# Column softmax with side projections in pieces of 128 columns, its sums copied one unit later, and the heads' inputs in another order with deeper rings

## The chip, the cores and the metric

One NeuronCore of one Trainium2 chip runs the whole program in one launch. The metric is the device time of one execution in microseconds; the time of a version is the median of its runs. Engines are named as in the profile: PE (TensorE, with PEld for its weight loads), DVE (VectorE), ACT (ScalarE), POOL (GpSimd) and SP (SyncE, here the queue that issues the DMAs).

## The reference, cut to what matters

Four transformer-like layers over `x` of 2 x 2048 tokens by 128 channels. The change touches two places of them.

```python
# layer 2: inputs of 16 heads of width 8, queries and keys rotated; six heads dot, four hyperbolic, six cosine
q = apply_rot(q, cos, sin); k = apply_rot(k, cos, sin)
tq = sqrt(1.0 / curv + sum(q * q, -1)); tk = sqrt(1.0 / curv + sum(k * k, -1))
qn = q / max(norm(q), 1e-12)

# layer 3, first part: a softmax over the QUERY axis, so that sums over keys are needed of its columns
scores = einsum('neax,nebx->neab', Q, K); A = softmax(scores, axis=2)
Out = einsum('neab,neax->neax', A, V)
# layer 3, second part: its projections need only xn
q = xn @ Wq; k, v = split(xn @ Wkv)
```

## The kernel before, in words

Activations stay in on-chip memory as [128 channels, 4096 tokens]. Each stage is a block in which every engine has its own list of instructions, and semaphores order them across engines. Within one engine the order is the order of the code, so an instruction that waits holds up all behind it.

**head_inputs** (from L973) makes layer 2's queries and keys: 2 jobs (q, k) of 8 chunks of 512 tokens, so 16 steps `n`. A step runs: PE projects twice (L1007, L1008); DVE rotates (L1066 to L1068); ACT squares (L1028); PE sums squares over a head (L1014); ACT takes a root by Ln and Exp (`time_of`, L1034, L1035); DVE clips (L1075); ACT takes the inverse root (`root`, L1039, L1040); DVE scales (L1080 to L1083). Then the float32 result is split in three bf16 parts: ACT copies the high part (L1044), DVE subtracts (`rests`, L1089), ACT copies the middle (L1049), DVE subtracts (`lows`, L1093). The same split of `time` runs on ACT (L1045, L1051) and POOL (L1104, L1108). The order on each engine is a software pipeline: in slot `k` an engine does, one behind the other, the listed parts, each for step `k - lag` (`slot`). Rings (`n % 4`, `n % 2`) hold the intermediate results, and waits on an older step guard them. SP stores q's parts when its 8 steps are done, and k's at the end.

**column_softmax_sums** (from L1726) treats 32 heads (2 batches x 16) of 16 tiles (`ST`). A tile is 128 keys against 2048 queries, in two units `h` of 1024 columns. For a unit PE makes scores (L1831, into a ring of three PSUM buffers, `RING`), DVE takes the negated maximum (L1964), ACT takes the exponential with its sum (L1885), and this frees the PSUM buffer. Eleven tiles later (`LAG`) PE adds the tile, weighted, into `r_ps` (`add_up`, L1842). After the 16 tiles of a head DVE copies `r_ps` out (`collect`, L1957), and the next head's first `add_up` waits for that copy. Per group of 8 tiles small operations of DVE, POOL and ACT make the weights (L1970, L1916 to L1924, L1951).

Between them PE makes, for one 128-token tile per head, three **side projections** (`side`, L1855 for kinds 0 and 1, L1858 for kind 2) for the second part of layer 3, into one PSUM bank of 512 columns. They stand behind tile 3, 8 and 13 of a head (`SIDE_AT`). ACT copies each out one tile later (L1892), SP stores them. PE's list for a tile is: scores of unit 0, scores of unit 1, `add_up`, and after three tiles a side projection.

Before the first head DVE clears `cs_q` and `cs_k` (L1941, L1942); SP waits for this before it loads the first heads (L1787). Of the 128 partitions 96 are then overwritten.

Of the kernel before, what the change touches and what calls it, by code (L numbers as in the profile page):

```python
# [972 lines left out]
def head_inputs(nc, xn, W, cos, sin, jobs):  # L973
# [7 lines left out]
    with Scope(nc, "hi") as sc:  # L981
        (projected, rotated, squared, summed, timed, clipped, rooted, scaled, act_step, high, rested, mid, low, t_high, t_rested, t_mid,
         t_low, stored, own) = (sc.sem(n) for n in names)
        a, time, f = (sc.sb(n, [128, 4, CH]) for n in ("a", "time", "f"))
# [15 lines left out]
        with nc.Block() as block:  # L1000
# [19 lines left out]
            def _(act):  # L1020
# [3 lines left out]
                def square(n):  # L1024
                    act.wait_ge(rotated, n + 1)
                    if n >= 2:
                        act.wait_ge(summed, n - 1)
                    act.activation(sq[:, n % 2, :], a[:, n % 4, :], ACT.Square).then_inc(squared, 1)  # L1028

                def time_of(n):  # L1030
                    act.wait_ge(summed, n + 1)
                    if n >= 4:
                        act.wait_ge(t_rested, n - 3)
                    steps(act.activation(time[:, n % 4, :], n_ps[:, n % 2, :], ACT.Ln, bias=W["inv_c"]))  # L1034
                    act.activation(time[:, n % 4, :], time[:, n % 4, :], ACT.Exp, scale=0.5).then_inc(timed, 1)  # L1035
# [6 lines left out]
                def highs(n):  # L1042
                    act.wait_ge(scaled, n + 1)
                    act.activation(part(parts, n, 0), a[:, n % 4, :], ACT.Copy).then_inc(high, 1)  # L1044
                    act.activation(part(t_parts, n, 0), time[:, n % 4, :], ACT.Copy).then_inc(t_high, 1)  # L1045
# [7 lines left out]
                for k in range(total + 4):  # L1053
                    slot(k, ((square, 0), (time_of, 1), (root, 2), (highs, 3), (mids, 4)))

            @block.vector
            def _(dve):
                steps = Steps(dve, own)

                def rotate(n):  # L1060
                    j, c = steps_of[n]
                    at = slice((c % CPB) * CH, (c % CPB + 1) * CH)
                    dve.wait_ge(projected, n + 1)
                    if n >= 4:
                        dve.wait_ge(rested, n - 3)
                    steps(dve.tensor_tensor(turned[:, n % 2, :], t_ps[:, n % 2, :], sin[:, at], ALU.mult))  # L1066
                    steps(dve.tensor_tensor(a[:, n % 4, :], a_ps[:, n % 2, :], cos[:, at], ALU.mult))
                    dve.tensor_tensor(a[:, n % 4, :], a[:, n % 4, :], turned[:, n % 2, :], ALU.add).then_inc(rotated, 1)  # L1068
# [8 lines left out]
                def scale(n):  # L1077
                    job = jobs[steps_of[n][0]]
                    if job["times_c"]:
                        steps(dve.tensor_scalar(time[:, n % 4, :], time[:, n % 4, :], W["c"], None, ALU.mult))  # L1080
                    dve.wait_ge(rooted, n + 1)
                    steps(dve.tensor_scalar(f[:, n % 4, :], f[:, n % 4, :], job["cosine"], job["base"], ALU.mult, ALU.add))
                    dve.tensor_tensor(a[:, n % 4, :], a[:, n % 4, :], f[:, n % 4, :], ALU.mult).then_inc(scaled, 1)  # L1083

                def rests(n):
# [3 lines left out]
                    dve.tensor_tensor(rest[:, n % 4, :], a[:, n % 4, :], part(parts, n, 0), ALU.subtract).then_inc(rested, 1)  # L1089
# [5 lines left out]
                for k in range(total + 4):  # L1095
                    slot(k, ((rotate, 0), (clip, 1), (scale, 2), (rests, 3), (lows, 4)))

            @block.gpsimd
            def _(pool):
                def rests(n):  # L1100
# [3 lines left out]
                    pool.tensor_tensor(t_rest[:, n % 4, :], time[:, n % 4, :], part(t_parts, n, 0), ALU.subtract).then_inc(t_rested, 1)  # L1104
# [5 lines left out]
                for k in range(total + 4):  # L1110
                    slot(k, ((rests, 3), (lows, 4)))
# [614 lines left out]
def column_softmax_sums(nc, qd, kd, r_dram, xn, side_weights, side_dram):  # L1726
# [8 lines left out]
    with Scope(nc, "cs") as sc:  # L1735
# [11 lines left out]
        SIDE_AT = (3, 8, 13)  # L1747
# [30 lines left out]
        with nc.Block() as block:  # L1778
            @block.sync
            def _(sp):  # L1780
# [23 lines left out]
                sp.wait_ge(cleared, 2)  # L1804
# [16 lines left out]
            def _(pe):  # L1821
# [25 lines left out]
                def side(seg, e, kind):  # L1847
                    if seg.it is not None or e or kind:
                        pe.wait_ge(side_copied, seg.count(3, 3 * e + kind))
                    if kind == 0:  # L1850
                        pe.wait_ge(side_staged, seg.count(1, e + 1))
                    tile = side_x[:, e % 2, :]
                    if kind < 2:
                        for j in range(4):
                            mm = pe.matmul(side_ps[:, j * 128:(j + 1) * 128], side_weights[kind][:, j * 128:(j + 1) * 128], tile,  # L1855
                                           start=True, stop=True)
                    else:
                        mm = pe.matmul(side_ps[:, :], tile, side_weights[2], start=True, stop=True)  # L1858
                    mm.then_inc(side_made, 1)

                def emit(seg):
                    for t in seg.tiles():
# [4 lines left out]
                        if t % ST in SIDE_AT:  # L1867
                            side(seg, t // ST, SIDE_AT.index(t % ST))
# [7 lines left out]
            def _(act):  # L1876
                def emit(seg):
                    for t in seg.tiles():
# [8 lines left out]
                        if t % ST - 1 in SIDE_AT:  # L1887
                            kind, e = SIDE_AT.index(t % ST - 1), t // ST
# [11 lines left out]
            def _(pool):  # L1900
                PER_GROUP = 1
# [38 lines left out]
            def _(dve):  # L1940
                dve.memset(q[:, :, :], 0.0).then_inc(cleared, 1)  # L1941
                dve.memset(k[:, :, :], 0.0).then_inc(cleared, 1)  # L1942
# [16 lines left out]
                def emit(seg):  # L1959
                    for t in seg.tiles():  # L1960
                        for h in range(2):
# [11 lines left out]
                            if t % ST == LAG - 1 and h == 0 and (seg.it is not None or t >= ST):  # L1973
# [649 lines left out]
```

## Time and profile before

| What | us |
|---|---|
| median of 3 runs | 7267.65 (7259.87 to 7271.13) |
| the profiled execution | 7271.85, its span 7270.1 |
| head_inputs, first DVE rotation to last subtraction | 2083.0 to 2232.6 of the span |
| column_softmax_sums, first scores to last copy of sums | 4187.3 to 5516.2 of the span |

The span is read in stages, since each has its own limit: the busy shares of a stage come from the table by stretches, the waits from the view of who waited for whom, and the order of single instructions from the timeline. A bracket at a timeline row's end is the idle time of that engine just before it, and what ended that. "x8" is a run of eight instructions merged in one row. Granted clock 1.0 is TensorE at 2.4 GHz, 0.5 at 1.2 GHz.

### The profile page before, as it was taken

To read this page: it belongs to the slowest core of one execution; us is meant where nothing else is said; L and a number is where in the kernel's file an instruction comes from. 1 tells how busy PE (TensorE), PEld (TensorE's weight loads), DVE (VectorE), ACT (ScalarE), POOL (GpSimd) and SP (SyncE) were. 2 spreads that over 40 slices of the span, in tenths; PEclk is the share of its full clock that TensorE was granted. 3 is DMA by queue.
4 is the path that set the end of the run, shared out by engine and by line. 5 is a ranking of instruction groups with operands and counts; after the bars stand their busy time and mean duration, and the time that the engine had idled before them with its cause. 6 is when DMAs were issued, how large, how long until landed. Compare 5 with 4: busy or idle time off the path is not lost. (4 is left out here: it accounts for less than half of the span.)

```text
span 7270.1 us, 82198 instructions
## 1 busy us (share of the span) xinstructions
PE 5207.4 (72%) x23371; PEld 1824.1 (25%) x23371; DVE 5160.6 (71%) x6074; ACT 3896.3 (54%) x5386; POOL 1562.8 (21%) x983
## 2 busy tenths in 40 slices
PE   5466677978854868833333367777775999999999
PEld 2122233433311222200000111111112344444443
DVE  4688845444455666489798489999994688888887
ACT  4333321242444534689799489999993333333333
POOL 0244400000011000000000000000000577777776
PEclk7678788988967988955555689999997999999999
DMA  0000000000003112000000233332331110111110
GB/s 17 4 0 0 0 13 12 0 15 0 0 16 106 34 29 51 17 11 0 13 0 0 73 36 41 38 43 36 44 36 21 44 30 21 24 30 30 30 30 12
DMA packets 204967, 174.58 MB, mean 24 GB/s; under 512 B 145346, under 2 KB 186446, under 8 KB 196526
## 3 DMA queue, kind: packets, MB, share of 16 engines
q1 hardware_dynamic: 204606, 170.09, 12.4%
q8 instruction: 187, 3.06, 0.2%
q14 instruction: 174, 1.43, 0.1%
HBM read 118.80 MB, written 51.23 MB: 23 GB/s over the span
## 5 line engine op out<-in xcount | busy, mean ns | idle before, releaser
L1964 DVE TENSOR_REDUCE cs_neg<-cs_s_ps 128x1 f32<-128x1024 f32 x1024 | 1182.4, 1215 | 112.2 <-PE cs_s_ps L1831 96.1
L1885 ACT ACTIVATE cs_E<-cs_s_ps,cs_neg 128x1024 f32<-128x1024 f32 x1024 | 1134.4, 1120 | 135.9 <-DVE cs_neg L1964 135.9
L2237 ACT ACTIVATE da_P<-da_P 128x1024 f32<-128x1024 f32 x512 | 541.2, 1057 | 930.9 <-DVE da_P L2312 912.1
L2278 POOL TENSOR_TENSOR da_psum<-da_psum,da_P 128x1024 f32<-128x1024 f32 x384 | 904.9, 2357 | 366.7 <-ACT da_P L2237 334.0
L2295 DVE TENSOR_REDUCE da_mx<-da_s_ps 128x1 f32<-128x1024 f32 x512 | 623.9, 1220 | 198.2 <-PE da_s_ps L2161 198.1
L1831 PE MATMUL cs_s_ps<-cs_q,cs_k 64*128 64x512 bf16 x2048 | 390.5, 396 | 372.2 <-ACT cs_E L1885 343.6
L1259 PE MATMUL hypb_o_ps<-hypb_P,hypb_vq 128*32 128x512 f32 (+3 forms) x640 | 193.7, 933 | 607.5 <-DVEq L1649 403.6
L2312 DVE TENSOR_TENSOR da_P<-da_s_ps,da_lift 128x1024 f32<-128x1024 f32 x512 | 600.6, 1215 | 3.5 <-PE da_s_ps L2165 3.4
L2161 PE MATMUL da_s_ps<-da_k,da_q 64*128 64x512 f32 x2048 | 553.1, 618 | 20.8 <-DMA da_v<-vf 15.2
L1842 PE MATMUL cs_r_ps<-cs_E,cs_w 128*32 128x512 f32 x4096 | 551.5, 613 | 1.4 <-POOL cs_w L1924 1.4
L2175 PE MATMUL da_o_ps<-da_P,da_v 128*64 128x512 f32 x2048 | 495.9, 605 | 0.0
L2165 PE MATMUL da_s_ps<-da_q,da_k 64*128 64x512 f32 x2048 | 482.9, 590 | 0.0
L478 PE MATMUL scan_y_ps<-scan_hC,consts 128*128 128x512 f32 x512 | 346.6, 814 | 145.5 <-POOL scan_hC L514 143.6
L514 POOL TENSOR_TENSOR scan_hC<-scan_h,scan_c_sb 128x1024 f32<-128x1024 f32 x128 | 301.2, 2353 | 642.6 <-DVE scan_h L537 642.6
L1461 DVE TENSOR_REDUCE cos_mu<-cos_m_ps 128x1 f32<-128x512 f32 (+1 forms) x480 | 262.3, 604 | 134.4 <-PE cos_m_ps L1420 91.4
L500 ACT ACTIVATE scan_dA<-mamba_dts,mamba_wt 128x1024 f32 x128 | 147.1, 1150 | 341.2 <-DVE scan_h L537 332.8
L1449 ACT ACTIVATE cos_P<-cos_s_ps 128x1024 f32<-128x1024 f32 (+1 forms) x240 | 203.6, 893 | 210.9 <-PE cos_s_ps L1398 118.3
L1831 PEld LDWEIGHTS cs_s_ps<-cs_q,cs_k 64*128 64x128 bf16 x2048 | 90.8, 93 | 884.3 <-ACT cs_E L1885 833.1
L1449 ACT ACTIVATE dot_P<-dot_s_ps 128x1024 f32<-128x1024 f32 (+1 forms) x240 | 202.0, 893 | 191.4 <-PE dot_s_ps L1398 124.2
L1104 POOL TENSOR_TENSOR hi_t_rest<-hi_time,hi_t_parts 128x512 f32<-128x512 f32 x16 | 20.8, 1300 | 1243.8 <-ACT hi_t_parts L1045 1243.7
L2165 PEld LDWEIGHTS da_s_ps<-da_q,da_k 64*128 64x128 f32 x2048 | 197.8, 187 | 240.0 <-issue 224.1
L1461 DVE TENSOR_REDUCE dot_mu<-dot_m_ps 128x1 f32<-128x512 f32 (+2 forms) x320 | 174.9, 605 | 103.0 <-PE dot_m_ps L1420 65.7
(437 smaller groups left out, 8904.0 us busy)
## 6 DMA issues: line engine op xcount, KB each, us to landing
da_q<-qf SPq DMA_DIRECT2D x32, 512.0 KB, 8.7
da_k<-kf SPq DMA_DIRECT2D x32, 512.0 KB, 10.6
cs_q<-q_parts SPq DMA_DIRECT2D x384, 32.0 KB
cs_k<-k_parts SPq DMA_DIRECT2D x384, 32.0 KB
qf<-cs_side_sb SPq DMA_DIRECT2D x32, 256.0 KB, 3.4
kf<-cs_side_sb SPq DMA_DIRECT2D x32, 256.0 KB, 5.3
vf<-cs_side_sb SPq DMA_DIRECT2D x32, 256.0 KB, 5.8
da_v<-vf SPq DMA_DIRECT2D x16, 512.0 KB, 11.9
```

Of the source, the lines that this page charges most:

```text
L1461: dve.tensor_reduce(mu[:, x % 2, i, o // CH:o // CH + 1], m_ps[:, u % M_RING, 0:w], AX.X, ext["op"]).then_inc(reduced, 1)
L1831: mm = pe.matmul(s_ps[:, seg.slot(u, RING, 2), c * CH:(c + 1) * CH], k[half, p, i * 128:(i + 1) * 128], q[half, p, at], start=True, stop=True)
L1842: mm = pe.matmul(r_ps[32 * a:32 * a + 32, :], weight, E[:, seg.slot(t, E_RING), a // 2, (a % 2) * CH:(a % 2 + 1) * CH], start=(i == 0), st ...
L1885: act.activation(E[:, seg.slot(t, E_RING), h, :], s_ps[:, seg.slot(u, RING, 2), :], ACT.Exp, bias=neg[:, g, j, h:h + 1], accum_out=z[:, g, ...
L1964: dve.tensor_reduce(neg[:, g, j, h:h + 1], s_ps[:, seg.slot(u, RING, 2), :], AX.X, ALU.max, negate=True).then_inc(maxed, 1)
L2161: mm = pe.matmul(s_ps[:, slot, c, :], q[half(c), p, tile * 128:(tile + 1) * 128], k[half(c), p, part * CH:(part + 1) * CH], start=True, st ...
L2165: mm = pe.matmul(s_ps[:, slot, c, :], k[half(c), p, kt * 128:(kt + 1) * 128], q[half(c), p, (quad % CPB) * CH:(quad % CPB + 1) * CH], star ...
L2175: mm = pe.matmul(o_ps[half(c), :], v[:, p, 2 * u + c, :], P[:, g % RING, c, :], start=(u == 0), stop=(u == UNITS - 1))
L2237: act.activation(P[:, g % RING, :, :], P[:, g % RING, :, :], ACT.Exp).then_inc(exped, 1)
L2278: pool.tensor_tensor(psum[:, :, :], psum[:, :, :], P[:, g % RING, :, :], ALU.add).then_inc(pooled, 1)
L2295: dve.tensor_reduce(mx[:, g // UNITS % 2, g % UNITS // 2, g % 2:g % 2 + 1], s_ps[:, slot, :, :].rearrange("p c n -> p (c n)"), AX.X, ALU.m ...
L2312: dve.tensor_tensor(P[:, g % RING, :, :], s_ps[:, slot, :, :], lift[:, quad % 2, :].unsqueeze(1).to_broadcast([128, 2, CH]), ALU.add).then ...
```

## The change

In head_inputs `a` gets 6 buffers for 4 and `time` 5 for 4, and the order within a slot and the lags change on ACT, DVE and POOL. In column_softmax_sums a side projection is made in pieces of 128 columns: one piece behind each of two tiles, two behind the third, so over tiles 3 to 5, 7 to 9 and 11 to 13. Kind 2, one matmul of 512 columns before, becomes four of 128. ACT copies the bank out in the tile of the last piece, no longer one tile later. DVE's `collect` moves behind the second unit of tile 10, from behind the first. The clearing takes only the partitions 32 to 63 and 96 to 127, `cs_q` by DVE and `cs_k` by POOL.

```diff
-        a, time, f = (sc.sb(n, [128, 4, CH]) for n in ("a", "time", "f"))
+        a, time, f = (sc.sb(n, [128, k, CH]) for n, k in (("a", 6), ("time", 5), ("f", 4)))
...
# ACT
-                for k in range(total + 4):
-                    slot(k, ((square, 0), (time_of, 1), (root, 2), (highs, 3), (mids, 4)))
+                for k in range(total + 5):
+                    slot(k, ((time_of, 1), (highs, 3), (square, 0), (mids, 5), (root, 1)))
...
# DVE
-                for k in range(total + 4):
-                    slot(k, ((rotate, 0), (clip, 1), (scale, 2), (rests, 3), (lows, 4)))
+                for k in range(total + 7):
+                    slot(k, ((rests, 4), (rotate, 0), (lows, 7), (clip, 1), (scale, 2)))
...
# POOL
-                for k in range(total + 4):
-                    slot(k, ((rests, 3), (lows, 4)))
+                for k in range(total + 2):
+                    slot(k, ((rests, 0), (lows, 2)))
...
-        SIDE_AT = (3, 8, 13)
+        SIDE_AT = {at + n: (kind, ((0,), (1,), (2, 3))[n]) for kind, at in enumerate((3, 7, 11)) for n in range(3)}
...
-                sp.wait_ge(cleared, 2)
+                sp.wait_ge(cleared, 4)
...
# PE
-                def side(seg, e, kind):
-                    if seg.it is not None or e or kind:
-                        pe.wait_ge(side_copied, seg.count(3, 3 * e + kind))
-                    if kind == 0:
-                        pe.wait_ge(side_staged, seg.count(1, e + 1))
+                def side(seg, e, kind, quarters):
+                    if quarters[0] == 0:
+                        if seg.it is not None or e or kind:
+                            pe.wait_ge(side_copied, seg.count(3, 3 * e + kind))
+                        if kind == 0:
+                            pe.wait_ge(side_staged, seg.count(1, e + 1))
                     tile = side_x[:, e % 2, :]
-                    if kind < 2:
...
-                    else:
-                        mm = pe.matmul(side_ps[:, :], tile, side_weights[2], start=True, stop=True)
-                    mm.then_inc(side_made, 1)
+                    for j in quarters:
+                        part = slice(j * 128, (j + 1) * 128)
+                        weight = side_weights[kind][:, part]
+                        mm = pe.matmul(side_ps[:, part], *((tile, weight) if kind == 2 else (weight, tile)), start=True, stop=True)
+                    if quarters[-1] == 3:
+                        mm.then_inc(side_made, 1)
...
# ACT, behind the two exponentials of tile t
-                        if t % ST - 1 in SIDE_AT:
-                            kind, e = SIDE_AT.index(t % ST - 1), t // ST
+                        if t % ST in SIDE_AT and SIDE_AT[t % ST][1][-1] == 3:
+                            kind, e = SIDE_AT[t % ST][0], t // ST
...
# POOL
+                for base in (32, 96):
+                    pool.memset(k[base:base + 32, :, :], 0.0).then_inc(cleared, 1)
+                pool.wait_ge(cleared, 4)
...
# DVE
-                dve.memset(q[:, :, :], 0.0).then_inc(cleared, 1)
-                dve.memset(k[:, :, :], 0.0).then_inc(cleared, 1)
+                for base in (32, 96):
+                    dve.memset(q[base:base + 32, :, :], 0.0).then_inc(cleared, 1)
...
-                            if t % ST == LAG - 1 and h == 0 and (seg.it is not None or t >= ST):
+                            if t % ST == LAG - 1 and h == 1 and (seg.it is not None or t >= ST):
```

How this moves instructions, at the places that matter. The first is PE's list round tiles 7 to 9 of the second head of column_softmax_sums, before (-) and now (+); L1831 are scores, L1842 is `add_up`, L1855 and L1857 are side projections (a row of four L1831 is one tile).

```order
 L1831 MATMUL cs_s_ps<-cs_q,cs_k 128x512 x4
 L1842 MATMUL cs_r_ps<-cs_E,cs_w 32x512 x4
+L1857 MATMUL cs_side_ps<-cs_side_x,l3w_wt 128x128
 L1831 MATMUL cs_s_ps<-cs_q,cs_k 128x512 x4
 L1842 MATMUL cs_r_ps<-cs_E,cs_w 32x512 x4
-L1855 MATMUL cs_side_ps<-cs_side_x,l3w_wt 128x128 x4
+L1857 MATMUL cs_side_ps<-cs_side_x,l3w_wt 128x128
 L1831 MATMUL cs_s_ps<-cs_q,cs_k 128x512 x4
 L1842 MATMUL cs_r_ps<-cs_E,cs_w 32x512 x4
+L1857 MATMUL cs_side_ps<-cs_side_x,l3w_wt 128x128 x2
```

Four matmuls in a row ahead of the next tile's scores have become one, one and two, behind three tiles. The second place is DVE in head_inputs, one slot of the k job in the middle of the stage. Before:

```order
L1066 TENSOR_TENSOR hi_turned<-hi_t_ps,l2p_sin 128x512
L1067 TENSOR_TENSOR hi_a<-hi_a_ps,l2p_cos 128x512
L1068 TENSOR_TENSOR hi_a<-hi_a,hi_turned 128x512
L1075 TENSOR_SCALAR hi_f<-hi_n_ps 128x512
L1082 TENSOR_SCALAR hi_f<-hi_f,l2w_wt 128x512
L1083 TENSOR_TENSOR hi_a<-hi_a,hi_f 128x512
L1089 TENSOR_TENSOR hi_rest<-hi_a,hi_parts 128x512
L1093 TENSOR_TENSOR hi_parts<-hi_rest,hi_parts 128x512
```

And now the same slot:

```order
L1089 TENSOR_TENSOR hi_rest<-hi_a,hi_parts 128x512
L1066 TENSOR_TENSOR hi_turned<-hi_t_ps,l2p_sin 128x512
L1067 TENSOR_TENSOR hi_a<-hi_a_ps,l2p_cos 128x512
L1068 TENSOR_TENSOR hi_a<-hi_a,hi_turned 128x512
L1093 TENSOR_TENSOR hi_parts<-hi_rest,hi_parts 128x512
L1075 TENSOR_SCALAR hi_f<-hi_n_ps 128x512
L1082 TENSOR_SCALAR hi_f<-hi_f,l2w_wt 128x512
L1083 TENSOR_TENSOR hi_a<-hi_a,hi_f 128x512
```

The instructions are the same eight. The clip L1075 is still one step behind the rotation, but ACT now begins its slot with that step's `time_of` and has no square of the newest step ahead of it; a step's last subtraction L1093 comes three slots later than before.

## Rows read from the trace of the kernel before

**Rows 1.** The page: busy us (share of the span) of each engine.
```profile
PE 5207.4 (72%) x23371; PEld 1824.1 (25%) x23371; DVE 5160.6 (71%) x6074; ACT 3896.3 (54%) x5386; POOL 1562.8 (21%) x983
```

**Rows 2.** Stretches: head_inputs, column softmax; us, busy PE, PEld, DVE, ACT, POOL, clock, DMA.
```profile
2082.00:2232.00 150.00, 69.41 (x94) 24.65 (x92) 113.89 (x136) 81.20 (x144) 43.85 (x31) 0.68 0.12 44
4188.00:5520.00 1332.00, 980.02 (x6718) 245.22 (x6714) 1210.31 (x1184) 1208.95 (x2208) 63.55 (x287) 0.98 0.30 39
```

**Rows 3.** Who waited for whom, 4210 to 5500 us: total us, times, longest.
```profile
DVE cs_neg L1964 <- PE cs_s_ps L1831: 73.0, 100, 3.4
...
DVE cs_r_sb L1957 <- PE cs_r_ps L1842: 14.8, 31, 0.5
```

**Rows 4.** Timeline of DVE over one head, 4600 to 4670 us: start, us, instruction, idle before.
```profile
4609.60 9.34 DVE L1964 TENSOR_REDUCE cs_neg<-cs_s_ps 128x1 f32<-128x1024 f32 x8 [0.79 <-PE cs_s_ps L1831]
...
4622.05 1.23 DVE L1964 TENSOR_REDUCE cs_neg<-cs_s_ps 128x1 f32<-128x1024 f32 x1 [0.63 <-PE cs_s_ps L1831]
...
4626.02 0.69 DVE L1957 COPY cs_r_sb<-cs_r_ps 128x512 f32<-128x512 f32 x1 [0.42 <-PE cs_r_ps L1842]
4626.63 8.00 DVE L1964 TENSOR_REDUCE cs_neg<-cs_s_ps 128x1 f32<-128x1024 f32 x7
4635.34 4.62 DVE L1964 TENSOR_REDUCE cs_neg<-cs_s_ps 128x1 f32<-128x1024 f32 x4 [0.70 <-PE cs_s_ps L1831]
...
4666.60 0.69 DVE L1957 COPY cs_r_sb<-cs_r_ps 128x512 f32<-128x512 f32 x1 [0.51 <-PE cs_r_ps L1842]
```

**Rows 5.** Timeline of PE round a side projection, same head.
```profile
4632.53 0.39 PE L1831 MATMUL cs_s_ps<-cs_q,cs_k 64*128 64x512 bf16 x2 [0.56 <-ACT cs_E L1885]
4632.85 1.06 PE L1842 MATMUL cs_r_ps<-cs_E,cs_w 128*32 128x512 f32 x8
4633.85 1.12 PE L1858 MATMUL cs_side_ps<-l3w_wt,cs_side_x 128*128 128x512 f32 x2
4634.91 0.61 PE L1831 MATMUL cs_s_ps<-cs_q,cs_k 64*128 64x512 bf16 x4
```

**Rows 6.** Timeline of ACT: a copy of a side projection and exponentials behind it.
```profile
4613.09 0.58 ACT L1892 ACTIVATE cs_side_sb<-cs_side_ps 128x512 f32<-128x512 f32 x1
4613.57 1.11 ACT L1885 ACTIVATE cs_E<-cs_s_ps,cs_neg 128x1024 f32<-128x1024 f32 x1
...
4614.66 1.12 ACT L1885 ACTIVATE cs_E<-cs_s_ps,cs_neg 128x1024 f32<-128x1024 f32 x1
```

**Rows 7.** Groups of DVE in head_inputs: busy, mean ns, idle before, releaser.
```profile
L1093 DVE TENSOR_TENSOR hi_parts<-hi_rest,hi_parts 128x512 bf16<-128x512 f32 x16 | 25.1, 1576 | 0.0
L1089 DVE TENSOR_TENSOR hi_rest<-hi_a,hi_parts 128x512 f32<-128x512 f32 x16 | 24.4, 1524 | 0.0
...
L1075 DVE TENSOR_SCALAR hi_f<-hi_n_ps 128x512 f32<-128x512 f32 x16 | 11.1, 691 | 29.0 <-ACT hi_time L1035 29.0
...
L1082 DVE TENSOR_SCALAR hi_f<-hi_f,l2w_wt 128x512 f32<-128x512 f32 x16 | 9.6, 597 | 4.3 <-ACT hi_f L1040 4.3
```

**Rows 8.** Timeline of head_inputs, DVE and POOL, one step; then DVE near the stage's end.
```profile
2149.56 1.27 POOL L1104 TENSOR_TENSOR hi_t_rest<-hi_time,hi_t_parts 128x512 f32<-128x512 f32 x1 [6.80 <-ACT hi_t_parts L1045]
2149.74 1.64 DVE L1089 TENSOR_TENSOR hi_rest<-hi_a,hi_parts 128x512 f32<-128x512 f32 x1
...
2150.80 1.59 POOL L1108 TENSOR_TENSOR hi_t_parts<-hi_t_rest,hi_t_parts 128x512 bf16<-128x512 f32 x1
2151.30 1.64 DVE L1093 TENSOR_TENSOR hi_parts<-hi_rest,hi_parts 128x512 bf16<-128x512 f32 x1
...
2228.81 0.68 DVE L1089 TENSOR_TENSOR hi_rest<-hi_a,hi_parts 128x512 f32<-128x512 f32 x1
```

**Rows 9.** Timeline: DVE's clearing, SP's first load behind it, a clearing by POOL.
```profile
4164.85 1.76 DVE L1942 MEMSET cs_k<- 128x2048 uint32 x1 [0.38 <-issue]
4166.64 0.32 SPq L1787 DMA_DIRECT2D cs_q<-q_parts  x1
...
2266.50 3.51 POOL L1375 MEMSET cos_vq<- 128x4096 f32 x1 [32.88 <-POOLq L957]
```

More of the change, by code:

```diff
@@ L1027, in square @@
                         act.wait_ge(summed, n - 1)
-                    act.activation(sq[:, n % 2, :], a[:, n % 4, :], ACT.Square).then_inc(squared, 1)
+                    act.activation(sq[:, n % 2, :], a[:, n % 6, :], ACT.Square).then_inc(squared, 1)
                 def time_of(n):
                     act.wait_ge(summed, n + 1)
[L1032 to L1035, printed above, removed]
+                    if n >= 5:
+                        act.wait_ge(t_rested, n - 4)
+                    steps(act.activation(time[:, n % 5, :], n_ps[:, n % 2, :], ACT.Ln, bias=W["inv_c"]))
+                    act.activation(time[:, n % 5, :], time[:, n % 5, :], ACT.Exp, scale=0.5).then_inc(timed, 1)
                 def root(n):
@@ L1043, in highs @@
                     act.wait_ge(scaled, n + 1)
-                    act.activation(part(parts, n, 0), a[:, n % 4, :], ACT.Copy).then_inc(high, 1)
-                    act.activation(part(t_parts, n, 0), time[:, n % 4, :], ACT.Copy).then_inc(t_high, 1)
+                    act.activation(part(parts, n, 0), a[:, n % 6, :], ACT.Copy).then_inc(high, 1)
+                    act.activation(part(t_parts, n, 0), time[:, n % 5, :], ACT.Copy).then_inc(t_high, 1)
                 def mids(n):
@@ L1079, in scale @@
                     if job["times_c"]:
-                        steps(dve.tensor_scalar(time[:, n % 4, :], time[:, n % 4, :], W["c"], None, ALU.mult))
+                        steps(dve.tensor_scalar(time[:, n % 5, :], time[:, n % 5, :], W["c"], None, ALU.mult))
                     dve.wait_ge(rooted, n + 1)
                     steps(dve.tensor_scalar(f[:, n % 4, :], f[:, n % 4, :], job["cosine"], job["base"], ALU.mult, ALU.add))
-                    dve.tensor_tensor(a[:, n % 4, :], a[:, n % 4, :], f[:, n % 4, :], ALU.mult).then_inc(scaled, 1)
+                    dve.tensor_tensor(a[:, n % 6, :], a[:, n % 6, :], f[:, n % 4, :], ALU.mult).then_inc(scaled, 1)
                 def rests(n):
@@ L1088, in rests @@
                         dve.wait_ge(low, n - 3)
-                    dve.tensor_tensor(rest[:, n % 4, :], a[:, n % 4, :], part(parts, n, 0), ALU.subtract).then_inc(rested, 1)
+                    dve.tensor_tensor(rest[:, n % 4, :], a[:, n % 6, :], part(parts, n, 0), ALU.subtract).then_inc(rested, 1)
                 def lows(n):
@@ L1103, in rests @@
                         pool.wait_ge(t_low, n - 3)
-                    pool.tensor_tensor(t_rest[:, n % 4, :], time[:, n % 4, :], part(t_parts, n, 0), ALU.subtract).then_inc(t_rested, 1)
+                    pool.tensor_tensor(t_rest[:, n % 4, :], time[:, n % 5, :], part(t_parts, n, 0), ALU.subtract).then_inc(t_rested, 1)
                 def lows(n):
@@ L1867, in emit @@
                         if t % ST in SIDE_AT:
-                            side(seg, t // ST, SIDE_AT.index(t % ST))
+                            side(seg, t // ST, *SIDE_AT[t % ST])
                 segments(pe, emit)
```

11 lines of the change are left out of this document (4 added, 7 removed).

## The prediction

> **What bounds the kernel now.** I read the page first: no engine is busy for more than 72% of the span [rows 1], so the limit changes from stage to stage, and only the two stages that the change edits matter. The table by stretches gives them [rows 2]. In column_softmax_sums DVE is busy for 1210.31 us and ACT for 1208.95 us of 1332, 91% each, and PE for 980.02. In head_inputs DVE is busy for 113.89 of 150 us, and the others for much less. So DVE is nearly the bound in both, and what can be won is its idle time, plus what lengthens its instructions.
>
> Next, the waits of column_softmax_sums [rows 3]: DVE waits 73.0 us for scores, in 100 waits, and 14.8 us in 31 waits ahead of its copy of the sums. The timeline says where [rows 4]. A head takes 40.58 us (from the copy at 4626.02 to the next at 4666.60), and DVE stops in it four times: 0.79, 0.63 and 0.70 us ahead of a maximum, one behind each side projection, and 0.42 to 0.51 us ahead of the copy. PE's timeline shows why [rows 5]: `add_up` holds it for 1.00 us (4632.85 to 4633.85), the side projection for 1.06 more, and only then can the scores of the next tile start.
>
> In head_inputs [rows 7] DVE waits 29.0 us ahead of the clip L1075, always for ACT's `time_of`, and 4.3 us ahead of L1082 for ACT's root. The subtractions L1089 and L1093 take 1.5 us each on average.
>
> **Part 1, the pieces.** A side projection delays the next scores by 1.06 us and costs DVE 0.71 us (mean of the three): 0.35 us are absorbed by the ring of three score buffers. Over 32 heads the three waits are 32 x 3 x 0.71 = 68 us; the 73.0 us [rows 3], less a few of other kinds, say the same. A quarter of a projection takes 1.06 / 4 = 0.265 us. A single piece is below the 0.35 absorbed and costs DVE nothing; what hides it is the time that the scores lie ready in the ring, and without that it would cost 0.265. Two pieces take 0.53 and leave 0.53 - 0.35 = 0.18 us. So three times 0.18 remain per head, 17 us in all, and the part gives 68 - 17 = **51 us**. Kind 2, cut from one matmul of 512 columns into four, has no row in that form; kinds 0 and 1 always had the form of four, and their waits (0.79, 0.63) stand beside the 0.70 of kind 2. So I take the same length. The number of PE's projections and their work stay as they are. The new matmuls wait for nothing new: kind 1 starts at tile 7 and kind 0 was copied behind tile 5.
>
> **Part 2, the sums one unit later.** At tile 10 DVE reaches the copy before PE has ended the `add_up` that it needs, since this stands in PE's list behind both scores of the tile. One unit of maximum takes 8.00 / 7 = 1.14 us [rows 4], more than the 0.42 to 0.51 us waited. The wait goes: 14.8 us x 32 / 31 = **15 us**. What is late next is PE's `add_up` of the next head's first tile, which waits for the copy; it stands behind both scores of tile 11, and these need the exponentials of tile 10, so it comes at about the time at which the copy ends. I cost it at nothing; without that cover it would cost up to the copy's 0.69 us less 0.35, 11 us in all.
>
> **Part 3, ACT's copy in the same tile.** The copy holds ACT for 0.48 us (4613.09 to 4613.57) [rows 6], and the scores behind it come later by that. It shows only as small gaps inside DVE's run: eight maxima in 9.34 us, from which (9.34 - 1.23) / 7 = 1.16 us each, against (8.00 - 1.23) / 6 = 1.13 where no copy lies [rows 4]. That is 0.2 us per copy, 20 us over 96 copies. Now it lies in the gap that the two last pieces leave. I take **8 us** of the 20. The new wait, of ACT for the last piece, has the next tile's exponentials behind it. From the scores of unit 1 the last piece ends 0.32 + 1.00 + 0.53 = 1.85 us later [rows 5]; a maximum (1.23) and an exponential (1.11) stand between those scores and the copy, so it waits for nothing.
>
> Together 51 + 15 + 8 = 74 us, 2.3 per head, to 38.3. The floor is DVE's own work per head: 32 maxima at 1.13, the copy 0.61 (4626.02 to 4626.63), and about 0.4 for the four small operations of the groups, 37.2 us. So these parts can give at most 3.4 x 32 = 109 us. At ACT's fastest pace, 1.09 us per exponential (4613.57 to 4614.66), it needs 34.9 + 3 x 0.48 + 0.3 = 36.6, so it does not bind before DVE. From below: if the ring absorbed nothing of a single piece and only 0.2 of a double one, the waits would be 3 x (0.265 x 2 + 0.33) = 2.6 per head, more than the 2.1 of now; parts 1 to 3 would give about 0. I take 74, since the 0.35 is measured on all three waits, and as the low end of the range half of it, 37.
>
> **Part 4, head_inputs.** The instructions are the same; the order changes. ACT now begins a slot with `time_of` of the last step, whose sum of squares is long there, and DVE clips it behind a rotation and two subtractions. So the 29.0 us go, and the 4.3 with them, since the root now has a whole slot. Against this stands the longer tail: the last subtraction comes 7 slots behind the rotation instead of 4, with little in each; three more slots of one 0.68 us subtraction [rows 8] come to 2 us. Gain 33.3 - 2.3 = **31 us** of 150. The two extra ring buffers pay for the longer lags and cost nothing by themselves. SP's stores of q start a few us sooner or later beside other work; those of k stay at the end as before.
>
> What POOL does to DVE stays open. L1089 takes 1.64 us while POOL's L1104 runs beside it, and 0.68 us where POOL is idle [rows 8]; the two subtractions thus lose 1.92 us a step, 31 us in all. In the new order POOL's two meet other instructions. I leave the loss as it is: the same POOL work meets a DVE that is now almost always busy. If it all fell on instructions that don't mind, the gain would be 31 + 31 = 62; if DVE stood still for all of POOL's 1.27 + 1.59 us a step [rows 8], the loss would grow by 0.94 x 16 = 15 us, and the gain fall to 16.
> The Trainium skill's page "SBUF — State Buffer" ("Who interferes with whom") says that a DVE instruction with two SBUF inputs and a GpSimd instruction that reads SBUF exclude each other for the whole instruction, while one with a single SBUF input is left alone. By that rule the L1066, L1067 and L1075, which read PSUM, would be free, and the sum would lie between those two ends. The trace agrees in the 1.64 against 0.68 us; that DVE gets something done within POOL's 2.84 us (2149.56 to 2152.39) speaks against a lock that is never yielded.
>
> **Part 5, the clearing.** DVE's two are as long as before if only the elements per partition count. POOL's have no row at 32 partitions in bf16. The nearest is 3.51 us for 4096 elements per partition [rows 9]; at that, two take 7.0 us from about 4162.9, and SP starts at 4170 in place of 4166.64: **+3.4 us**, on the path, since PE waits for these loads. If bf16 went at twice the rate it would be 0. As nothing in the trace excludes a gain, the lower end is -1.8, one of DVE's 1.76 us.
>
> **Sum:** -74 - 31 + 3.4 = -102 us, so 7271.85 - 102 = 7170 for a profiled execution. The median before is 4.2 us below that execution, so I forecast 7166.
>
> **The rivals.**
> (a) *The floor comes sooner.* Column softmax gains 37 us, because ACT, as busy as DVE, takes over the waits, or because single pieces aren't absorbed. For: 91% busy on both [rows 2]. Against: ACT's pace of 1.09 us behind a copy. Time: -37 - 31 + 3.4 = -65, 7203. Chance 0.14.
> (b) *POOL locks DVE.* DVE stands for all of POOL's 2.86 us a step, since its six instructions on on-chip data alone meet them: -74 - 16 + 3.4 = -87, 7181; chance 0.12, as DVE was seen to get on beside POOL. It is what the rule of the Trainium skill's page "SBUF — State Buffer" would come to at its strictest.
>  The mirror case, POOL's work meeting free instructions: -74 - 62 + 3.4 = -133, 7135; chance 0.08.
> (c) *Slower: each change of PE from `add_up` to a piece has a fixed price.* If what costs DVE 0.71 us is not the projection's length but the interruption, nine tiles cost 6.4 us per head where three cost 2.1: +137 us, less 15 and 31, plus 3.4: +94, 7362. It decides from the point where 9 x 32 x w - 68, with w the wait per tile with a piece, exceeds 15 + 31 - 3.4, that is from w = 0.38 us. Against: PE goes from `add_up` to L1858 and on to the scores without idle [rows 5]. Chance 0.03.
> (d) *It doesn't do what it says:* the sides' gaps stay, as the clip's wait moves to another instruction of DVE and the double pieces to the old wait; within 0.2% of now. Chance 0.03.
>
> The forecast itself, with part 1 to 3 between 55 and 95 and part 4 between 22 and 45, has 0.60, and reaches from 7133 to 7194. The range takes in (b) whole and most of (a): 7130 to 7205. Faster by over 0.2% (14.5 us, about what a measurement of this kernel can tell from no change) has 0.94, within it 0.03, slower 0.03.
>
> **What would show it.** Right: a head of 38.3 us from copy to copy; no idle above 0.1 us behind tiles 3, 4, 7, 8, 11 and 12, and about 0.2 behind 5, 9 and 13; none ahead of the copy of sums; in head_inputs no wait of DVE at the clip, and a stage of 119 us for 149.6; SP's first load 7 us behind the start of the clearing. Wrong: heads of 39.5 us or more with waits spread over nine tiles, a wait of PE at `add_up` for the copy, or a DVE in head_inputs that is busy throughout but with more instructions at 1.6 us.

## The result, and the profile after

The changed kernel takes 7211.99 us (median of 4 runs, 7206.25 to 7221.84), the kernel before beside it 7263.76: a ratio of 0.9933, 95% interval 0.9913 to 0.9952. That is faster, by 52 us, but only half of the forecast 102, and outside the range. (One of the nine executions of the kernel before beside runs 11 and 12 took 14498.82 us, at a granted clock of 0.415, and is in no ratio.) The profiled executions differ by 7270.1 - 7219.8 = 50.3 us of span. Cut at the first and last instructions on each stage's tiles, the difference is:

| stretch | before | after | difference | forecast |
|---|---|---|---|---|
| start to head_inputs | 2083.0 | 2087.2 | +4.2 | 0 |
| head_inputs, to the last use of its parts | 157.1 | 121.5 | -35.6 | -31 |
| from there to the clearing | 1922.6 | 1913.4 | -9.2 | 0 |
| clearing to the first scores | 24.6 | 26.8 | +2.2 | +3.4 |
| first scores to last copy of sums | 1329.0 | 1270.7 | -58.3 | -74 |
| to the first scores of dense_attention | 146.3 | 150.9 | +4.6 | 0 |
| scores of dense_attention | 1583.5 | 1625.3 | **+41.8** | 0 |
| tail | 24.0 | 24.0 | 0 | 0 |

dense_attention, which the diff does not touch, gives back 42 us. The first line of part 1 of the page, and the instruction queue in part 3 (187 packets before):

```profile
PE 5250.3 (73%) x23563; PEld 1868.7 (26%) x23563; DVE 5158.4 (71%) x6074; ACT 3904.0 (54%) x5386; POOL 1568.6 (22%) x985
...
q8 instruction: 192, 3.15, 0.2%
```

The page counts 192 matmul records more for PE [rows 1]: kind 2 is now four matmuls in place of one, so three more in each of 32 heads, and each is two records. The list of who waited for whom, PE from 5500 us on, has a line that is missing before:

```profile
PE da_s_ps L2164 <- issue: 33.3, 9, 6.5
```

Here are its two costliest places in one pass of the loop, in PE's timeline (start, us, instruction, idle before):

```profile
6184.32 1.13 PE L2164 MATMUL da_s_ps<-da_k,da_q 64*128 64x512 f32 x4 [2.29 <-issue]
6185.28 1.89 PE L2168 MATMUL da_s_ps<-da_q,da_k 64*128 64x512 f32 x8
6193.63 2.08 PE L2164 MATMUL da_s_ps<-da_k,da_q 64*128 64x512 f32 x4 [6.46 <-issue]
```

The same pair stands at 6392.66 and 6401.98, at 6600.97 and 6609.46, and at 6808.75 and 6817.80: at four of the loop's five back-edges, at its head and again 12 matmul records later. PE waits there for nothing that the profile shows; the experiments say for what. The stretch table adds the clock (columns: us, busy PE, PEld, DVE, ACT, POOL, granted clock, DMA share, GB/s):

```profile
6170.00:6182.00 12.00, 12.00 (x57) 4.56 (x55) 10.05 (x12) 4.61 (x5) 9.34 (x5) 1.00 0.02 3
6192.00:6196.00 4.00, 2.37 (x6) 0.80 (x8) 0.25 (x1) 0.00 (x0) 1.99 (x1) 0.50 0.90 201
```

Behind the idle time the clock is at 0.50, 1.2 GHz, and the four records of L2164 take 2.08 us for 1.13. So 33.3 of the 41.8 us are the waits, and the clock behind them makes up the rest: over the four pairs, the rows that ran at the low clock in whole or in part (L2164, L2168, L2178) are 9.6 us longer than the same rows at 1.00, which would make 42.9. The 0.90 of DMA share is the loads of the next head, which SP starts at the same place.

The column softmax, DVE over one head (answers to [rows 4]):

```profile
4644.04 0.68 DVE L1960 COPY cs_r_sb<-cs_r_ps 128x512 f32<-128x512 f32 x1
4644.64 11.78 DVE L1967 TENSOR_REDUCE cs_neg<-cs_s_ps 128x1 f32<-128x1024 f32 x10
...
4660.06 10.38 DVE L1967 TENSOR_REDUCE cs_neg<-cs_s_ps 128x1 f32<-128x1024 f32 x9
4670.74 4.62 DVE L1967 TENSOR_REDUCE cs_neg<-cs_s_ps 128x1 f32<-128x1024 f32 x4 [0.29 <-PE cs_s_ps L1831]
...
4680.40 2.36 DVE L1967 TENSOR_REDUCE cs_neg<-cs_s_ps 128x1 f32<-128x1024 f32 x2 [0.23 <-PE cs_s_ps L1831]
4682.68 0.68 DVE L1960 COPY cs_r_sb<-cs_r_ps 128x512 f32<-128x512 f32 x1
```

A head takes 38.64 us from copy to copy, for 40.58 before. Of the four waits two are left in this view, of 0.29 and 0.23 us, and none ahead of the copy. (The view shows no wait under 0.15 us; the single records have three more, of 0.13, 0.07 and 0.07.) DVE's groups in head_inputs (answers to [rows 7]; one of the 16 L1068 lies ahead of the view):

```profile
L1089 DVE TENSOR_TENSOR hi_rest<-hi_a,hi_parts 128x512 f32<-128x512 f32 x16 | 19.6, 1224 | 0.1
L1068 DVE TENSOR_TENSOR hi_a<-hi_a,hi_turned 128x512 f32<-128x512 f32 x15 | 18.3, 1220 | 0.5
L1093 DVE TENSOR_TENSOR hi_parts<-hi_rest,hi_parts 128x512 bf16<-128x512 f32 x16 | 15.4, 979 | 0.0
L1083 DVE TENSOR_TENSOR hi_a<-hi_a,hi_f 128x512 f32<-128x512 f32 x16 | 14.5, 904 | 0.5
L1075 DVE TENSOR_SCALAR hi_f<-hi_n_ps 128x512 f32<-128x512 f32 x16 | 10.9, 680 | 1.7 <-ACT hi_time L1035 1.7
```

The clip's wait is 1.7 us, for 29.0 before. POOL's two groups there:

```profile
L1108 POOL TENSOR_TENSOR hi_t_parts<-hi_t_rest,hi_t_parts 128x512 bf16<-128x512 f32 x16 | 24.3, 1523 | 22.5 <-ACT hi_t_parts L1051 22.5
L1104 POOL TENSOR_TENSOR hi_t_rest<-hi_time,hi_t_parts 128x512 f32<-128x512 f32 x16 | 19.6, 1225 | 1185.2 <-ACT hi_t_parts L1045 1185.2
```

In the clearing (answers to [rows 9]) SP starts its first load 6.6 us behind DVE's start, when POOL's two are done. Before, it started 1.79 us behind the start of DVE's second.

```profile
4121.65 7.06 POOL L1902 MEMSET cs_k<- 32x4096 bf16 x2 [603.46 <-POOLq L227]
4122.13 1.76 DVE L1945 MEMSET cs_q<- 32x2048 uint32 x1 [20.48 <-PEq L227]
...
4128.74 0.32 SPq L1787 DMA_DIRECT2D cs_q<-q_parts  x1
```

### The profile page after: what moved, and what is told of

Its sections match the earlier page's. It is cut to its first block and busy times, and to the rows that moved or that the text cites. A ratio compares the mean times of both kernels' runs of the same rounds, so it can differ in the third digit from the quotient of the medians.

```text
span 7219.8 us, 82581 instructions
## 1 busy us (share of the span) xinstructions
PE 5250.3 (73%) x23563; PEld 1868.7 (26%) x23563; DVE 5158.4 (71%) x6074; ACT 3904.0 (54%) x5386; POOL 1568.6 (22%) x985
## 5 line engine op out<-in xcount | busy, mean ns | idle before, releaser
L2164 PE MATMUL da_s_ps<-da_k,da_q 64*128 64x512 f32 x2048 | 558.5, 623 | 51.8 <-issue 33.3
L1831 PE MATMUL cs_s_ps<-cs_q,cs_k 64*128 64x512 bf16 x2048 | 402.5, 397 | 263.0 <-ACT cs_E L1885 221.3
L1842 PE MATMUL cs_r_ps<-cs_E,cs_w 128*32 128x512 f32 x4096 | 552.6, 613 | 2.5 <-POOL cs_w L1927 0.9
L2178 PE MATMUL da_o_ps<-da_P,da_v 128*64 128x512 f32 x2048 | 500.1, 609 | 0.0
L2168 PE MATMUL da_s_ps<-da_q,da_k 64*128 64x512 f32 x2048 | 483.5, 590 | 0.0
L1104 POOL TENSOR_TENSOR hi_t_rest<-hi_time,hi_t_parts 128x512 f32<-128x512 f32 x16 | 19.6, 1225 | 1185.2 <-ACT hi_t_parts L1045 1185.2
L1831 PEld LDWEIGHTS cs_s_ps<-cs_q,cs_k 64*128 64x128 bf16 x2048 | 98.2, 93 | 638.9 <-ACT cs_E L1885 562.8
L2168 PEld LDWEIGHTS da_s_ps<-da_q,da_k 64*128 64x128 f32 x2048 | 198.2, 187 | 241.0 <-issue 225.1
```

The costliest lines, as they stand in the source:

```text
L1831: mm = pe.matmul(s_ps[:, seg.slot(u, RING, 2), c * CH:(c + 1) * CH], k[half, p, i * 128:(i + 1) * 128], q[half, p, at], start=True, stop=True)
L1842: mm = pe.matmul(r_ps[32 * a:32 * a + 32, :], weight, E[:, seg.slot(t, E_RING), a // 2, (a % 2) * CH:(a % 2 + 1) * CH], start=(i == 0), st ...
L2164: mm = pe.matmul(s_ps[:, slot, c, :], q[half(c), p, tile * 128:(tile + 1) * 128], k[half(c), p, part * CH:(part + 1) * CH], start=True, st ...
L2168: mm = pe.matmul(s_ps[:, slot, c, :], k[half(c), p, kt * 128:(kt + 1) * 128], q[half(c), p, (quad % CPB) * CH:(quad % CPB + 1) * CH], star ...
L2178: mm = pe.matmul(o_ps[half(c), :], v[:, p, 2 * u + c, :], P[:, g % RING, c, :], start=(u == 0), stop=(u == UNITS - 1))
```

## The experiments

**Theory A:** the extra matmuls lengthen PE's instruction list by 96 instructions, all ahead of dense_attention's loop (the program text holds 8 of the 32 heads, so 24 matmuls more, each of two weight loads and two matmul records in the trace). They so shift that loop, whose body is 2094 instructions (928 matmul records and 1166 others of PE in one pass), against the blocks in which instructions are fetched. A slot is the place of the loop's first instruction in a block, taken to be 256 instructions. **B:** something else of the change, its timing, buffers or clock. **C:** chance.

**1 and 2. Empty instructions.** `for _ in range(n): pe.nop(nofuse=True)` ahead of `heads(pe, emit)`, 96 in the kernel before and 160 in the changed one.

> The kernel before with 96 empty instructions on PE ahead of dense_attention's program, as many as the change puts there. Measured: the stretch from the last copy of sums in column_softmax_sums to the end of the span, 1754.6 us before and 1801.0 us after the change. Theory A (the longer instruction list of PE shifts the loop of dense_attention against the blocks in which instructions are fetched): 1801 us, with idle PE 'issue' times of 2 and 6 us per iteration at L2164. Theory B (the change's own timing, buffers or the clock do it) and theory C (chance of one run): 1755 us and none of these waits.

> The changed kernel with 160 empty instructions on PE ahead of dense_attention's program, so that with the 96 of the change its loop is moved by 256. Theory A, if the blocks hold 256 instructions: the stretch behind column_softmax_sums is back at about 1755 us, no issue waits at L2164, and the kernel takes 7212 - 46 = 7166 us. Theories B and C: 1801 us or any value between, and 7212 us.

Measured: 7250.69 us and 7206.65 (ratio 0.9931, 0.9906 to 0.9956). The empty instructions were dropped in the build, as the pages' counts show (82198 and 82581 instructions, as without them), so both runs are repeats and no test of A. They rule out C: dense_attention's scores took 1583.3 us and 1622.6, with 187 and 192 packets in the instruction queue, as in the two first profiles.

**3. Kind 2 whole.**

```
-                    for j in quarters:
-                        part = slice(j * 128, (j + 1) * 128)
+                    for j in [j for j in quarters if kind < 2 or j == 0]:
+                        part = slice(j * 128, (j + 1) * 128) if kind < 2 else slice(0, CH)
...
-                    if quarters[-1] == 3:
+                    if quarters[-1] == 3 if kind < 2 else quarters[0] == 0:
```

> The changed kernel with the third side projection left whole, one matmul of 512 columns at tile 11, so that PE's list is as long as before the change. Theory A: stretch behind column_softmax_sums 1755 us. Theory B, if it is anything but the length of PE's list: 1801 us. In the column softmax a head should be 0.5 to 0.7 us longer than the 38.64 us of the change, since the wait of 0.7 us for the whole projection is back and the 0.2 us of the double piece is gone.

Measured: 7164.83 us (one run), dense_attention 1583.1, 187 packets. The stalls are gone with the 96 instructions. The surprise is in the column softmax: its stretch is 1270.4 us, as with the pieces (1266.8 to 1270.7), the head 38.71 us. DVE there:

```profile
4670.53 0.68 DVE L1960 COPY cs_r_sb<-cs_r_ps 128x512 f32<-128x512 f32 x1
4671.12 2.34 DVE L1967 TENSOR_REDUCE cs_neg<-cs_s_ps 128x1 f32<-128x1024 f32 x2
4673.84 9.15 DVE L1967 TENSOR_REDUCE cs_neg<-cs_s_ps 128x1 f32<-128x1024 f32 x8 [0.37 <-PE cs_s_ps L1831]
```

At tile 11 the whole projection costs DVE 0.37 us, where it cost 0.70 at tile 13 before [rows 4]; two reasons are likely, and neither was tested apart: DVE has just spent 0.6 us on the copy of sums, and ACT's copy of the projection stands two tiles behind it here, for one tile before. Cutting kind 2 gained 0.08 us a head, under 3 us, and cost 42.

**4. head_inputs alone**, in the kernel before.

> The kernel before with head_inputs alone as changed. head_inputs from first rotation to last subtraction: 113.9 us, as in the changed kernel, for 149.6. Everything behind it as before: 1930 us from there to the clearing, head of 40.5 us, 1755 us behind the column softmax. If part of the 9 us that the changed kernel wins between head_inputs and the clearing comes from head_inputs (where its last stores stand), it is here too: 1921 us.

Measured: 7222.85 us (one run), head_inputs 121.4 us to the last use of its parts (121.5 after, 157.1 before), heads and dense_attention as before (1333.3, 1583.2). From head_inputs to the clearing 1910.1: across all runs this unchanged stretch lies between 1904.9 and 1922.6, with and without the change, so the 9.2 us there are no more than the spread between runs.

**5, 6 and 7. The loop's place set by hand.**

```
         def heads(eng, emit, emit_at=None):
             emit(0, True, False)
+            if emit_at is not None:
+                eng.addr_align(256, offset=emit_at, max_nops=0)
             with eng.Fori(1, NH3 - 1) as it:
```

> The 96 and 160 empty instructions of the two runs before were dropped when the kernels were built, so those runs were repeats. Here PE's loop of dense_attention in the kernel before is put at slot 222 of 256, where by the length of PE's list the change has put it (its body is 2094 instructions; from slot 222 it ends in a tenth block of 256, from slots up to 210 in the ninth). Theory A (placement): issue waits of 2 and 6 us per iteration at L2161, stretch behind column_softmax_sums about 1795 to 1801 us for 1754.6, kernel 7257 + 40 to 46 = 7297 to 7303 us. Theory B (anything else of the third projection's four pieces): 1755 us, 7257.

> The changed kernel with PE's loop of dense_attention put at slot 64 of 256. Theory A: no issue waits at L2164, stretch behind column_softmax_sums 1755 us for 1801, kernel 7209 - 42 = 7167 us. Theory B: the four pieces of kind 2 cost it wherever the loop stands: 1795 to 1801 us, 7209.

Measured: the changed kernel with its loop at 64 takes **7165.27 us** (ratio 0.9851, 0.9834 to 0.9868; dense_attention 1582.8); the kernel before with its loop at 222 takes 7265.13 beside 7262.89 (1.0003, 0.9991 to 1.0015; 1589.8), a miss: its dense_attention is only 6.3 us longer, with one issue wait of 1.85 us, behind the last back-edge. So a shift of the loop cures the changed kernel, pieces and all, but I had the wrong place. The second stall itself tells the place: it comes behind 12 matmul records, 25 to 28 instructions behind the loop's head, so that by theory A a block ends there.

> In the changed kernel the second stall stands 25 to 28 instructions behind the loop's head, so a boundary of 256 lies there and the head at slot 230, not 222 as assumed in the run before. Here the loop of the kernel before is put at slot 230. Theory A (placement alone): an issue wait of 2 us at the head and of up to 6 us behind the first 12 matmuls, in most iterations, first scores to last scores of dense_attention 1623 to 1625 us for 1583.5, one instruction packet more per back-edge (192 or 193 for 187). Theory B (the four pieces or the aligned loop itself do it, and 64 only helped by its jump): 1583 to 1590 us, 188 packets.

Measured: 7296.86 us (one run; before 7260.62), dense_attention 1627.5, 191 packets, and the stalls, now in the kernel before (PE's timeline):

```profile
6260.06 1.13 PE L2163 MATMUL da_s_ps<-da_k,da_q 64*128 64x512 f32 x4 [2.74 <-issue]
6268.99 1.01 PE L2167 MATMUL da_s_ps<-da_q,da_k 64*128 64x512 f32 x1 [6.10 <-issue]
```

Nothing of the change is in this kernel, and its dense_attention loses 44 us, the kernel 36. Theory A is shown from both sides; B falls.

**8, 9 and 11. The column softmax taken apart**, all with the loop at 64: the first hunk, the second, and both.

```
-                            if t % ST == LAG - 1 and h == 1 and (seg.it is not None or t >= ST):
+                            if t % ST == LAG - 1 and h == 0 and (seg.it is not None or t >= ST):
...
-                        if t % ST in SIDE_AT and SIDE_AT[t % ST][1][-1] == 3:
-                            kind, e = SIDE_AT[t % ST][0], t // ST
+                        if t % ST - 1 in SIDE_AT and SIDE_AT[t % ST - 1][1][-1] == 3:
+                            kind, e = SIDE_AT[t % ST - 1][0], t // ST
```

> The changed kernel with PE's loop at slot 64, and the copy of the sums back in the first unit of tile 10. By part 2 of the prediction: the wait of DVE ahead of the copy is back, 0.4 to 0.5 us per head, and the stretch from first scores to last copy of column_softmax_sums is 1268 + 15 = 1283 us. Rival: the wait was slack that the ring of scores takes up, 1268 to 1271 us.

> The changed kernel with PE's loop at slot 64, and ACT's copy of a side projection one tile behind its last piece, as it was. By part 3: 8 us more in the same stretch, 1276 us. Rivals: no difference (1268 us), since ACT's own time is the same wherever the copy stands; or the whole 20 us, 1288.

> The changed kernel with PE's loop at slot 64, the copy of the sums back in the first unit of tile 10 and ACT's copy back one tile behind the last piece: of the change to the column softmax only the pieces are left. Putting either back alone cost 10.7 and 11.6 us (1278.9 and 1279.8 for 1268.2). If the two don't meet: first scores to last copy 1290 to 1291 us, and the pieces are worth 1330 - 1290 = 40 us, not the 51 of part 1. If they share a wait: 1280 to 1286, and the pieces are worth 45 to 50.

| in the kernel | stretch, us | head, us | kernel, one run |
|---|---|---|---|
| all three parts (run 6) | 1268.2 | 38.63 | 7165.27 (median of 4) |
| sums in the first unit (8) | 1278.9 | 38.91 | 7176.33 |
| ACT's copy a tile later (9) | 1279.8 | 38.94 | 7193.70 |
| pieces alone (11) | 1318.8 | 40.18 | 7220.03 |
| none (before; runs 1, 4, 5, 7) | 1328.8 to 1333.3 | 40.57 | 7257.18 to 7265.99 (medians of before in the five comparisons) |

The stretch of the same column softmax differs by up to 4.5 us between profiles (1328.8 to 1333.3), so the 11 us of runs 8 and 9, one profile each, are rough; by the heads they are 32 x 0.28 = 9 and 32 x 0.31 = 10 us. The parts do not add up. Pieces alone are worth some 12 us, not 40 to 50; with either of the others some 50, with both 62. What the two moves are worth without the pieces was not run. Run 11's waits of PE, 4210 to 5420 us, and its timeline say why:

```profile
PE cs_s_ps L1831 <- ACT cs_E L1885: 192.0, 325, 2.8
PE cs_side_ps L1857 <- ACT cs_side_sb L1892: 44.7, 59, 1.6
```

```profile
4743.06 1.06 PE L1842 MATMUL cs_r_ps<-cs_E,cs_w 128*32 128x512 f32 x8
4745.37 0.49 PE L1857 MATMUL cs_side_ps<-l3w_wt,cs_side_x 128*128 128x128 f32 x2 [1.25 <-ACT cs_side_sb L1892]
4745.79 0.39 PE L1831 MATMUL cs_s_ps<-cs_q,cs_k 64*128 64x512 bf16 x2
```

With pieces in nine tiles the next kind starts two tiles behind the last, and a copy one tile later is not yet done when PE gets there; the next scores then stand behind the waiting piece. This wait is 44.7 us in run 11, 6.9 in run 9, and absent in runs 6 and 8. In run 9 DVE no longer stops ahead of the sums; that this is what shortens the wait there was not shown further.

**10. Twelve single pieces.**

```
-        SIDE_AT = {at + n: (kind, ((0,), (1,), (2, 3))[n]) for kind, at in enumerate((3, 7, 11)) for n in range(3)}
+        SIDE_AT = {at + n: (kind, (n,)) for kind, at in enumerate((2, 7, 12)) for n in range(4)}
```

> The changed kernel with PE's loop at slot 64, and the sides in twelve single pieces, kinds at tiles 2 to 5, 7 to 10 and 12 to 15. If single pieces are absorbed and the double ones leave 0.23 to 0.37 us each (about 0.9 per head), a head takes 38.64 - 0.9 = 37.8 us and the kernel 7165 - 28 = 7137. Rival: ACT, or PE's total work, is then the bound and the head stays above 38.3: 7154 or more. Rival: each piece costs something of its own, head of 38.6 or longer.

Measured: 7179.91 us (ratio 0.9883, 0.9866 to 0.9899), head 38.71: no gain. The number fits both rivals. Against PE's total work as the bound speaks that PE still waits 180.0 us for ACT (4210 to 5420 us). For a cost of each piece speak DVE's stops, now behind the first pieces of kinds 0 and 1:

```profile
4668.50 11.58 DVE L1967 TENSOR_REDUCE cs_neg<-cs_s_ps 128x1 f32<-128x1024 f32 x10 [0.25 <-PE cs_s_ps L1831]
4680.59 3.49 DVE L1967 TENSOR_REDUCE cs_neg<-cs_s_ps 128x1 f32<-128x1024 f32 x3 [0.31 <-PE cs_s_ps L1831]
```

A bound in ACT was not tested apart. The same single piece leaves 0.07 us behind tile 3 of the changed kernel and 0.25 behind tile 2 here, so what the ring absorbs is not the same at each tile. PE's timeline of run 11 shows the lengths of a single and a double piece, each to the start of the scores behind it:

```profile
4736.85 0.49 PE L1857 MATMUL cs_side_ps<-cs_side_x,l3w_wt 128*128 128x128 f32 x2
4737.27 0.39 PE L1831 MATMUL cs_s_ps<-cs_q,cs_k 64*128 64x512 bf16 x2
...
4739.15 0.71 PE L1857 MATMUL cs_side_ps<-cs_side_x,l3w_wt 128*128 128x128 f32 x4
4739.79 0.82 PE L1831 MATMUL cs_s_ps<-cs_q,cs_k 64*128 64x512 bf16 x4
```

A single piece holds PE for 0.42 us and a double for 0.64, and so they do in the changed kernel (medians of 192 and 96). A quarter thus costs 0.22, and each visit 0.2 more; four in one visit took 1.09 in the kernel before.

**12. A version that beats both:** the loop at 64, a hint for the back-edges of the column softmax's loop on each engine, and the clearing as it was before the change.

```
-            with eng.Fori(0, N_LOOP) as it:
+            with nc.Fori(0, N_LOOP, engines=[eng.engine], hint_back_edge=True) as it:
```

> The changed kernel with PE's loop of dense_attention at slot 64, a prefetch hint for the back-edges of the loop in column_softmax_sums on all five engines, and the clearing of q and k as it was before the change. If the 3 to 7 us by which a head at a back-edge is longer are instruction fetch that a hint can hide: those four heads come down from 43 to 44 us to 39 or 40, 15 to 18 us less in the stretch (1250 to 1253 for 1268). Rival: only DVE's two issue waits of 4 us or nothing go, 1260 to 1268. Clearing to first scores: 20.4 us for 23.0. Kernel: 7165 - 3 - 16 = 7146, or 7155 to 7162 by the rival.

Measured: **7153.30 us** (5 runs, 7135.06 to 7165.19; ratio 0.9837, 0.982 to 0.9855). The stretch is 1252.4 us, and the longest head takes 39.40 us; in run 6 the four at the back-edges took 42.82 to 43.94. In run 6 DVE's waits, 4210 to 5400 us, had an issue line:

```profile
DVE cs_neg L1967 <- issue: 8.5, 2, 4.4
```

Now they have none:

```profile
DVE cs_neg L1964 <- PE cs_s_ps L1831: 18.0, 64, 0.7
DVE cs_r_sb L1957 <- PE cs_r_ps L1842: 7.7, 1, 7.7
DVE cs_total L1951 <- POOL cs_total L1920: 2.0, 1, 2.0
```

The stretch came as expected; the kernel is 7 us above the 7146 and inside neither of the two forecasts. Clearing to first scores is 21.8 us, for 22.5 to 23.6 in the experiments with the changed clearing and 20.0 to 20.7 in those without; expected were 20.4.

## Why the prediction was wrong

**The step that failed** is the first one, "only the two stages that the change edits matter". It priced what the edited instructions do and not what their number does to code behind them: +41.8 us in dense_attention. No rival covered it. With the loop shifted back, the same change takes 7165.27 us, against 7166 forecast. That agreement is partly luck. The gain beside its own kernel before is 7262.89 - 7165.27 = 97.6 us for 102, and that kernel before was 4.8 us faster than the one the forecast started from. And two terms missed in opposite directions, parts 1 to 3 and part 4:

**Parts 1 to 3** were 74 us; they are 1330.6 - 1268.6 = 62 (means of the stretch in five runs with the old order, before and runs 1, 4, 5 and 7, and in three with the new, after and runs 2 and 6). The head was 38.64, not 38.3. By single records (medians over the heads) DVE's idle times before were 0.79, 0.63, 0.71 and 0.50 us, much as read. Left of them are 0.29, 0.22 and 0.13 behind the double pieces, 0.07 behind the single ones of tiles 3 and 12, and nothing behind the other four: 0.78 in all, where 3 x 0.18 = 0.54 was forecast. The mis-sized term is the length of a piece: "1.06 / 4 = 0.265 us" for a single one and 0.53 for a double, where 0.42 and 0.64 were measured. This is (0.78 - 0.54) x 32 = 8 of the 12 us that are missing. The absorbed 0.35 us is right for one double piece (0.64 - 0.35 = 0.29), and too small for the others. Some 3 us more are a stop's own price: undisturbed maxima of 1.215 us start every 1.131, and each stop loses that overlap of 0.08 as well; there are five stops now, for four. Rival (a), a gain of 37 us, fell with the 62. Rival (c) had a price per visit; PE pays one, 0.2 us, but what DVE loses is 0.78 + 5 x 0.08 = 1.2 us a head over nine tiles, 0.13 each, far below the 0.38 from which it would have decided.

**The split into 51, 15 and 8** was wrong too. The sentence "The new matmuls wait for nothing new" holds for the change as a whole, but not for the pieces alone (run 11); one of the two moved copies, of the sums or of the projection, is a condition of part 1, and the second is worth some 11 us more. The "0.2 us per copy, 20 us over 96 copies" of part 3 was misread: the single records show such a gap once a head, at tile 7, where two maxima start 1.32 us apart for 1.13. It is gone now, 6 us for the 8 that were taken; part 3 itself, run 9 against run 6, was worth 11.6 us.

**Part 2** was right in its mechanism: no wait ahead of the copy. It was worth 10.7 us (run 8, one run) for 15.

**Part 4** gave 35.6 us for 31. The clip's wait went from 29.0 to 1.7 us, that of L1082 from 4.3 to 0.3. What POOL takes from DVE shrank too: over the 0.68 us of an undisturbed instruction the four groups above lose 16 x (0.54 + 0.30 + 0.22) + 15 x 0.54 = 25 us, where L1089 and L1093 alone lost 16 x (0.84 + 0.90) = 28. It moved in part to the addition L1068 and the product L1083. Rival (b), DVE standing for all of POOL's work, fell: POOL is busy for 24.3 + 19.6 = 44 us there, and the part gained more than forecast, not less.

**Part 5**: +2.2 us in the profiled pair and +2.8 between the means of the experiments (20.3 and 23.1) for the forecast 3.4. POOL's 3.5 us per clearing of 4096 elements was right.

## What to carry to other kernels

Count the instructions that a change adds ahead of a long loop, on each engine, and look in the trace of the changed kernel for "issue" waits at back-edges of stages that the diff does not name; if they are there, set the loop's place before judging the change (a hint at the back-edge was tried here on another loop alone, where it helped). Split work on a busy engine only as finely as the slack needs, since each visit has its own price and each split adds instructions. Test the parts of a change together as well as apart: here pieces alone were worth 12 us, and the same pieces with either copy moved some 50.

## What the runs showed of the hardware

- **A loop's place in the instruction fetch.** The loop of dense_attention on PE runs in 1582.8 to 1585.6 us at slots 64 and, by the 96 instructions between the lists, 134; in 1589.8 at 222; and in 1622.6 to 1627.5 at 230. A packet of the instruction queue is 3.06 MB / 187 = 16.4 KB, and the stalled kernels fetch more of them: 192 for 187 with five back-edges, 191 for 188 in the placed ones. The Trainium skill's page "Runtime: NRT & Kernel Launch" ("Instruction fetch mechanics") says that fetch comes in blocks of 16 KiB or 256 instructions, that PE holds 2048, and that a taken branch to a block outside the current window stalls. The trace agrees with the stalls and the packet size. By that rule alone a body of 2094 would stall at every back-edge and every place. At 64 and 134 no issue wait is seen, and at 222 one, of 1.85 us at one back-edge of five; from which slot on it stalls at nearly all is known only as between 222 and 230. By counting blocks it should have been 211. Why it is not, stays open.
- **Two stalls, not one:** 2.3 to 2.7 us at the head and 2.9 to 6.8 at the next block (at the first back-edge the head's is missing, and in the changed kernel the other is only 0.64). The loads of the next head fill the DMA engines in all of these second stalls, the short ones too (share 0.95 or more), so that they do not tell short from long. Whether the loads lengthen them was not tested.
- **A back-edge hint works on the loop of the column softmax:** the four heads of about 43 us are gone and the stretch is 16 us shorter (1252.4 for 1268.2).
